# Graph loads one by one, score halves next to each other, three per-graph VectorE operations made per-group GpSimd operations, and separate orders for the first and last group

## The reference

```python
# layer 0
h = x @ W + b;  h = adj @ h / adj.sum(-1)
# layer 1: one weight per node, softmax over the nodes of a graph
w = (q * (adj @ (k * mask))).sum(-1) / sqrt(256);  out = softmax(w)[:, None] * v
# layer 2: attention, 8 heads of 32; the mask is adj + adj
scores = q @ k.T * 32 ** -0.5 * (adj + adj);  out = softmax(scores) @ v @ Wo.T + bo
# layer 3: two hypergraph convolutions, a ReLU and a normalisation between
H = (adj != 0)
m = Be[:, :, None] * (H^T @ (x @ W^T));  out = Dn[:, :, None] * (H @ m) + b
```

## Time and profile before

| | us |
|---|---|
| Median of 3 runs | 1978.1 (1973.22 to 1980.12) |
| Profiled execution | 1963.71 |
| Its span, first to last instruction | 1962.0 |
| PE busy in the span | 1873.0 |
| DVE busy | 1714.7 |
| ACT busy | 1478.6 |
| POOL busy | 1265.0 |

### The profile page before, as it was taken

The page is one execution under the profiler, slowest core; times in us unless marked ns, Lnnn a source line. Parts: engine busy times, 40 slices in busy tenths (PEclk is TensorE's granted clock), DMA queues, the critical chain, the costliest instruction groups (busy, mean ns, idle before and its releaser), DMA issues.

```text
span 1962.0 us, 53573 instructions
## 1 busy us (share of the span) xinstructions
PE 1873.0 (95%) x15357; PEld 1630.5 (83%) x15357; DVE 1714.7 (87%) x4867; ACT 1478.6 (75%) x4431; POOL 1265.0 (64%) x2568
## 2 busy tenths in 40 slices
...
DMA packets 57546, 46.14 MB, mean 24 GB/s; under 512 B 5168, under 2 KB 56880, under 8 KB 57520
## 3 DMA queue, kind: packets, MB, share of 16 engines
...
q10 hardware_dynamic: 1760, 1.90, 0.3%
...
## 4 chain that ended last, share of the span: by engine, by line
PE 78%; DMA 5%; issue 5%; DVE 4%; POOL 4%; ACT 2%; SPq 1%; DVEq 0%; POOLq 0%; ACTq 0%
PE ps L340 38%; PE ps L403 7%; PE ps L443 6%; PE ps L411 6%; DMA a_in<-in_adj_dram 4%; PE ps L419 4%; PE ps L324 4%; PE ps L432 4%; PE ps L356 3%; PE ps L392 3%; POOL ln_rs L653 2%; PE ps L350 1%; DVE x2T L732 1%; PE ps L330 1%; ACT y_out L508 1%
## 5 line engine op out<-in xcount | busy, mean ns | idle before, releaser
L564 ACT ACTIVATE z<-z,z_max 128x128 f32<-128x128 f32 x1024 | 399.1, 398 | 7.2 <-DVE z_max L840 3.1
L653 POOL TENSOR_TENSOR ln_rs<-ln_ve,minus_half 128x1 f32<-128x1 f32 x640 | 360.8, 564 | 50.2
L674 POOL TENSOR_TENSOR z<-z,z_rcp 128x1024 f32<-128x1024 f32 x128 | 242.8, 1897 | 192.9 <-DVE z_rcp L847 192.9
L651 POOL TENSOR_TENSOR ln_ve<-ln_mv,eps_col 128x1 f32<-128x1 f32 x640 | 131.1, 205 | 192.7 <-DVE ln_mv L722 192.7
L656 POOL TENSOR_SCALAR ln_nm<-ln_mv,ln_rs 128x1 f32<-128x1 f32 x640 | 179.7, 281 | 109.8 <-POOL ln_rs L653 109.8
L829 DVE SCALAR_TENSOR_TENSOR z<-ps,a_hold 128x256 f32<-128x256 f32 x512 | 190.5, 414 | 61.4 <-PE ps L403 56.7
L340 PE MATMUL ps<-w1T,txT 128*128 128x512 f32 x768 | 205.0, 402 | 1.0 <-DVE txT L732 1.0
L340 PE MATMUL ps<-w2T,mnT 128*128 128x256 f32 x1536 | 202.3, 284 | 0.1
L564 ACT ACTIVATION_READ_ACCUMULATOR z<-z,z_max 128x1 f32 x1024 | 199.7, 195 | 0.0
L340 PEld LDWEIGHTS ps<-w2T,mnT 128*128 128x128 f32 x1536 | 185.6, 189 | 0.3 <-issue 0.3
L840 DVE TENSOR_REDUCE z_max<-z 128x4 f32<-128x512 f32 x256 | 172.3, 673 | 2.2
(11 more groups left out here) (149 smaller groups left out, 5092.4 us busy)
## 6 DMA issues: line engine op xcount, KB each, us to landing
x_in<-in_x_dram SPq DMA_DIRECT2D x32, 512.0 KB, 4.0
out_dram<-y_out SPq DMA_DIRECT2D x128, 128.0 KB, 1.7
a_in<-in_adj_dram SPq DMA_DIRECT2D x32, 256.0 KB, 2.8
x<-in_L_gnn_Wqk_dram ACTq DMA_DIRECT2D x1, 512.0 KB, 5.6
h<-in_L_gnn_W_dram SPq DMA_DIRECT2D x1, 512.0 KB, 5.3
h<-in_L_gnn_W_dram ACTq DMA_DIRECT2D x1, 512.0 KB, 10.4
v<-in_L_gnn_Wo_dram SPq DMA_DIRECT2D x1, 256.0 KB, 6.2
b_all<-in_L_gnn_b_dram SPq DMA_DIRECT2D x2, 128.0 KB, 8.2
```

Source lines behind the costliest of these rows:

```text
L564: m = act.activation(z[:, g % 2, h, :], z[:, g % 2, h, :], ACT.Exp, bias=z_max[:, g % 2, h:h + 1], accum_out=z_sum[:, g % 2, h:h + 1])
L651: pool.tensor_tensor(ve[n][:, g:g + 1], mv[n][:, g, 1:2], eps_col[:, :], ALU.add).then_inc(eps_made[n], 1)
L653: pool.tensor_tensor(rs[n][:, g:g + 1], ve[n][:, g:g + 1], minus_half[:, :], ALU.pow).then_inc(root_made[n], 1)
L674: pool.tensor_tensor(zg, zg, z_rcp[:, g % 2, :].unsqueeze(2).to_broadcast([P, HEADS, P]), ALU.mult)\
```

## The change

Inputs and the copy of adj are loaded with one DMA for each graph: four for adj (64 KB each), four for x (128 KB each), and four that bring adj a second time, twice over, into `a_hold` with its new form of two equal halves, so that DVE makes no copy. In a round SP issues 16 DMAs, before 6. The score products run with c outside and k inside, and in the new order of PE `sc0` and `sc1` of graphs 0, 1 and 3 stand directly behind each other. DVE reads one half out of PSUM with one instruction over 512 elements. Masking, scaling and the mask's own copy become one GpSimd instruction for a group each (`am`, `hb`, `mask`), and GpSimd makes a constant of the residual for a group with two instructions over 1024 elements (`c3`); DVE's `x3b` is then one instruction for a graph. All orders are new; `v2.0` moves from the end of a round into the next one, `mp.0` to `mp.2` to its start, and `hyper` from its end to its middle. The first and the last group have orders and banks of their own.

The core of the diff:

```diff
     "pe": """
-        at.0+:3 at.1+:6 at.2+:2 sc0.0:0 mp.0:3 ax.0+:4 ax.1+:5 at.3+:7 sc1.0:2 v2.1:6 sc1.1:0 ax.2+:7
...
+        mp.0:7 mp.1:0 mp.2:1 at.0+:6 sc0.0:4 sc1.0:2 at.1+:0 at.2+:6 at.3+:1 ax.0+:7 ax.1+:0 v2.0:1 sc0.1:3
+        sc1.1:5 h0.0+:2 mp.3:7 ax.2+:3 sc0.2:5 ax.3+:7 v2.1:0 h0.1+:4 pt.0:1 h0.2+:3 sc1.2:4 cx.0:6 x1t.0+:1
...
-ORDER = {engine: steps(text) for engine, text in ORDER_TEXT.items()}
-FIRST = {engine: [s for s in schedule if s[2] == 1] for engine, schedule in ORDER.items()}
-LAST = {engine: [s for s in schedule if s[2] == 0] for engine, schedule in ORDER.items()}
+ORDER, FIRST, LAST = ({engine: steps(text) for engine, text in texts.items()}
+                      for texts in (ORDER_TEXT, FIRST_TEXT, LAST_TEXT))
...
             def load_a(q, g):
-                after(sp, made["at"], q * G)
+                after(sp, made["at"], before(q, g, G))
                 after(sp, a_summed, q)
-                after(sp, a_held, q)
-                sp.dma_start(a_in[:, :, :], adj_d[bass.ds(q * G, G)].rearrange("g n m -> n g m")).then_inc(a_loaded, 16)
+                sp.dma_start(a_in[:, g, :], adj_d[bass.ds(q * G + g, 1)].rearrange("g n m -> n (g m)")).then_inc(a_loaded[g], 16)
+
+            def load_hold(q, g):
+                after(sp, read["sc0"], before(q, g, G))
+                after(sp, read["sc1"], before(q, g, G))
+                sp.dma_start(a_hold[:, g, :, :], adj_d[bass.ds(q * G + g, 1)].rearrange("g n m -> n g m").to_broadcast([P, C, P]))\
+                    .then_inc(hold_loaded[g], 16)
...
             def sc(half):
                 def stage(q, g, o, b):
-                    if g == 0:
-                        for s in ("q0", "q1", "k0", "k1"):
-                            pe.wait_ge(read[s], q + 1)
-                    for k in range(RG // 2):
-                        r = half * RG // 2 + k
-                        at_ = slice(r * HD, (r + 1) * HD)
-                        for c in range(C):
+                    for s in ("q0", "q1", "k0", "k1"):
+                        pe.wait_ge(read[s], q + 1)
+                    for c in range(C):
+                        for k in range(RG // 2):
+                            r = half * RG // 2 + k
+                            at_ = slice(r * HD, (r + 1) * HD)
                             m = pe.matmul(ps[:, b + k, c * P:(c + 1) * P], qT[at_, c, g * P:(g + 1) * P],
                                           kT[at_, c, g * P:(g + 1) * P], start=True, stop=True)
...
+            def am(q, g):
+                pool.wait_ge(mask_made, q + 1)
+                pool.wait_ge(read["at"], nth(q, G - 1))
+                after(pool, made["amx"], q * G)
+                pool.tensor_tensor(amT[:, :, :], aT[:, :, :], mask[:, :].unsqueeze(2).to_broadcast([P, G, P]), ALU.mult)\
+                    .then_inc(amT_made, 1)
...
+            def c3_(q, g):
+                pool.wait_ge(d_made, q * 2 + 2)
+                after(pool, x3b_made, q * G)
+                pool.tensor_tensor(c3[:, :, :], bw_all[:, :].unsqueeze(1).to_broadcast([P, G, D]),
+                                   d_cnt[:, :].unsqueeze(2).to_broadcast([P, G, D]), ALU.mult).then_inc(c3_half, 1)
+                pool.wait_ge(c3_half, q + 1)
+                pool.tensor_tensor(c3[:, :, :], c3[:, :, :], b2_all[:, :].unsqueeze(1).to_broadcast([P, G, D]), ALU.add)\
+                    .then_inc(c3_made, 1)
...
             def asum(q, g, o):
-                dve.wait_ge(a_loaded, q * 16 + 16)
-                after(dve, wm_made, q)
-                dve.tensor_copy(mask[:, :], maskT[:, bass.ds(q * G, G)]).then_inc(mask_made, 1)
+                for k in range(G):
+                    dve.wait_ge(a_loaded[k], q * 16 + 16)
...
+                    dve.scalar_tensor_tensor(out=z[:, g % 2, hs, :].rearrange("p (r c) n -> p r (c n)", r=RG // 2),
+                                             in0=ps[:, b:b + RG // 2, 0:C * P], scalar=HC,
+                                             in1=a_hold[:, g, :, :].rearrange("p c n -> p (c n)").unsqueeze(1)
+                                             .to_broadcast([P, RG // 2, C * P]),
+                                             op0=ALU.mult, op1=ALU.mult).then_inc(read[f"sc{half}"], 1)
...
-            def x3c_(q, g, o):
-                dve.wait_ge(x3b_made, nth(q, g))
-                dve.wait_ge(d_made, q * 2 + 2)
-                dve.scalar_tensor_tensor(out=x3b[:, g, :], in0=bw_all[:, :], scalar=d_cnt[:, g:g + 1], in1=x3b[:, g, :],
+            def x3b_(q, g, o):
+                dve.wait_ge(norm_made["ln2"], nth(q, g))
+                dve.wait_ge(c3_made, q + 1)
+                after(dve, norm_made["ln4"], before(q, g, G))
+                dve.scalar_tensor_tensor(out=x3b[:, g, :], in0=x3[:, g, :], scalar=2.0, in1=c3[:, g, :],
                                          op0=ALU.mult, op1=ALU.add).then_inc(x3b_made, 1)
```

More of the change, by code:

```diff
@@ L56 @@
+        q1.0+ ln4_norm.3
     """,
     "dve": """
-        asum.0+ sc0.0 zmax0.0 sc1.0 zmax1.0 ax_lo.0+ sc1.1 ax_lo.1+ zmax1.1 zrcp.0 sc0.1 h0.0+ zmax0.1
-        ax_lo.2+ ln0_stats.0+ h0.1+ ln0_aggr.0+ ln0_stats.1+ sc0.2 zrcp.1 sc1.2 zmax0.2 ax_lo.3+ cx_lo.0
-        h0.2+ ln0_aggr.1+ zmax1.2 wo.0 ln0_stats.2+ ln2_stats.0 ln2_aggr.0 sc0.3 am.0+ sc1.3 zrcp.2 h0.3+
-        x1t_lo.0+ zmax0.3 am.1+ ln0_aggr.2+ ln0_stats.3+ tx_lo.0 dinv.0 ln0_aggr.3+ zmax1.3 cx_lo.1 am.2+
-        xg.0+ h1.0 x1t_lo.1+ wo.1 zrcp.3 am.3+ cx_lo.2 hold.0+ ln2_stats.1 xg.1+ ln2_aggr.1 x1t_lo.2+ wo.2
@@ L68 @@
-        x2t_lo.1+ y.2 x2t_lo.2+ ln4_stats.2 x2t_lo.3+ ln4_aggr.2 y.3 ln4_stats.3 ln4_aggr.3 hyper.0+
+        asum.0+ z0.0 zmax0.0 z1.0 ax_lo.0+ zmax1.0 z0.1 z1.1 zmax1.1 zrcp.0 ax_lo.1+ zmax0.1 h0.0+
+        ln0_stats.0+ ax_lo.2+ h0.1+ ln0_aggr.0+ z0.2 zrcp.1 h0.2+ zmax0.2 ln0_stats.1+ ln0_stats.2+ ax_lo.3+
+        ln0_aggr.1+ z1.2 cx_lo.0 h0.3+ x1t_lo.0+ ln0_aggr.2+ zmax1.2 wo.0 ln2_stats.0 ln0_stats.3+
+        ln2_aggr.0 z1.3 ln0_aggr.3+ z0.3 zmax1.3 xg.0+ zrcp.2 dinv.0 x1t_lo.1+ cx_lo.1 zmax0.3 x1t_lo.2+
@@ L541, in aT_free @@
                 after(act, made["ax"], before(q, g, G))
-                after(act, amT_made, before(q, g, G))
+                after(act, amT_made, q)
                 after(act, hT_made, q)
```

253 lines of the change are left out of this document (149 added, 104 removed).

## The result

| | median of the runs | span profiled | granted clock |
|---|---|---|---|
| before | 1975.66 us (1965.51 to 1980.12, 4 runs) | 1962.0 | 0.986 |
| changed | 2017.3 us (2016.75 to 2019.3, 4 runs) | 2017.6 | 0.980 |

The ratio is 1.022, 95% interval 1.0178 to 1.0262. The kernel is slower, where 1952 us and a gain of 1.3% were predicted, and the time lies outside the range. The two profiled spans lie 56 us apart and the medians 42, since the profiled execution of the kernel before is faster than its median.

The account below looks back on a forecast made before the run. PE's own queue was taken to set the pace of a round. Minus 0.75 us a round over 31 rounds (minus 23) and minus 3 at the ends took 1978.1 to 1952 us, range 1892 to 1996.

Parts of the forecast that it names:

- From `cx.0` to the next s: Rest of a round until the next first adj load issue (s): same work less two `mp` and a wait, 42.95 us.
- it only makes waits rarer: DVE loses at least 3 of its 53.06 us a round; nothing needs that, as PE is the longer one.
- the race of POOL for `probs.3`: `probs.3` queued behind `c3` on POOL comes 0.3 to 1.3 us late for `pt.3`; taken as 0.
- the 58.15 forecast: Length of a round: 15.2 us to `cx.0` plus 42.95 after it, 0.75 us less than before.
- Landings of 1.9 and 2.2 us: At a round's start, small loads take 1.9 us for 64 KB and 2.2 us for 128 KB, by slope.
- the 2.15 us of the other estimate: 64 KB load time by the skill page's fit; each landing 0.25 us later, 8 us in all.
- the stretch that the prediction summed: Round's start on PE, 4.6 us with 2.7 of work: some 1.9 us idle, against 0.8 in the old order.
- Minus 1.2 us of PE work a round: Score halves on PE: three pairs and two single halves take 3.40 us, where the old order took 4.60.
- the term is wrong: Sign for the score pairs: a pair taking 1.1 us or more would refute the 1.2 us saving.
- Rival 3: `probs.3` or a normalisation root behind `c3` or `hb` on POOL comes 1.5 us late for PE: 1998 us, chance 0.08.
- The ends: Filling and draining parts: minus 1 and minus 2 us, minus 3 in all; bounds plus 3 and minus 10.
- rival 2: Granted clock falls in more rounds, 4.6 us each; six more cancel the gain, ten more give 1998 us; chance 0.17.

Follow-up runs that it names:

- part 2: `hyper` moved to the end of DVE's round, `hb.0` last on POOL, against the changed kernel: 1972.0 us; with `d_inv` early too, 1968.45 us.
- part 1: Against the changed kernel: `d_inv` one place earlier on DVE, 2003.8 us; `hyper` behind `ln2_aggr.3`, 2019.07 us; both, 2018.39 us.
- the kernel of 1968: Changed kernel with `d_inv` one place earlier, `hyper` at the end of DVE's round and `hb.0` last on POOL: 1968.45 us.
- Part 5: Three score pairs taken apart: changed kernel 2217.54 us; with `d_inv` early, `hyper` last, one adj load 2094.75; that load also issued by ScalarE 1965.46.

## Why the prediction was wrong

**The step that failed** is "From `cx.0` to the next s ... The new order has there the same work": 42.95 us were forecast. The rows have 61.13 - 15.09 = 46.04. The two stretches, before and after, in the columns of the earlier trace rows:

```profile
1036.76:1080.28 43.52, 43.15 (x364) 38.29 (x364) 41.58 (x122) 33.65 (x92) 33.83 (x73) 1.00 0.03 10
1057.69:1103.73 46.04, 43.48 (x362) 38.35 (x361) 40.08 (x112) 34.42 (x92) 31.13 (x66) 1.00 0.04 13
```

The prediction took the 58.9 of one round and the `cx.0` of another, which has 43.5 behind it and not 43.9, so its 42.95 should have been 42.6. Of the missing 3.5 us three waits make 2.55: 1.45 ahead of `xg.1`, 0.84 ahead of `xg.3`, 0.26 ahead of `cx.3`. Most of the remainder is work: PE is busy there for 0.33 us more than before, where 0.66 less were forecast; why is open.

That step stood on the sentence that DVE loses work and "it only makes waits rarer". DVE did lose 3 us a round and its waits grew, for two reasons. The change takes `hyper` from the end of DVE's round, where DVE waits for the next loads anyway, to its full middle; the prediction used `hyper` only in the race of POOL for `probs.3` and never asked what stood behind it on DVE. That is 45 us by part 2. And it priced DVE and POOL as if each were alone, while `d_inv` and `hb` come to stand beside POOL's 1.9 and 2.4 us instructions. For `d_inv` that is some 0.8 us of an undisturbed round by part 1, of which falls of the clock took back about half, and 0.2 or nothing once `hyper` is out of the way; freeing `hb` alone gave nothing. The earlier trace rows held the sign: `hb`'s L804 took 744 ns for 128 elements, longer than the 0.68 us of a reduction over 512. In the trace all but four of the 128 take 0.7 to 0.8 us, beside POOL's `x2c` of 0.73 us; the four of the filling part take 0.28. I copied the mean as a price and did not ask why.

With both out of the way (the kernel of 1968) an undisturbed round still takes 59.4 us, 1.2 more than the 58.15 forecast. Half of that is the 0.6 us at `pt.3`, the term that the prediction worked out as POOL being late by 0.3 to 1.3 us and then took as 0. The rest was not traced.

**The loads.** Landings of 1.9 and 2.2 us were forecast, 1.8 and 2.1 came, so not the 2.15 us of the other estimate either; `cx.0` at s + 15.2 was 15.09. The waits of PE in the stretch that the prediction summed are 1.1 us and not 1.9, and three `mp` take 0.81 us, not 0.65 (by its own 0.33 for one they should have been 0.99), but neither sets `cx.0`: the chain through DVE and ScalarE does, as it had worked out. What it did not ask is what this start would take with one load, all else as changed: taking the split back gives 35 us, of which falls of the clock, two in place of fifteen, are some 7. The split itself was no gain, since `a_sum` waits for all four loads and heads DVE's order, while x is issued behind them.

**The pairs.** The term "Minus 1.2 us of PE work a round" was for two pairs more than before. Part 5 takes three pairs apart: 2.0 and 1.9 us, where the prediction's rows make 1.8. So the price of a pair holds. In the changed kernel less of it is seen: a new pair holds PE for 1.01 or 1.07 us to the next start, the third for 0.67, and with two halves alone, 0.65 each, that is 4.05 us by the time line of that round against the 4.60 of before; PE's busy time in a round fell by 0.1 us. The rows of 1.08 and 1.14 us were also the sign that was to mean "the term is wrong", and it was a bad sign: no other part that was tested costs as much when it is taken back (200 us on the changed kernel, against 106 for `c3`). Why the experiments give a pair more than its rows is open.

**POOL and fill and drain.** `c3` takes 4.3 us in one piece (3.8 to 4.8 forecast), and `pt.3` did not wait for POOL in the changed kernel, but only because PE was held up ahead of it. Rival 3 had the sign right with the wrong chain, POOL holding DVE and not PE. The ends were forecast at minus 3 and gave minus 8.6 in the span; undoing their orders costs 12.

**The clock (rival 2).** Fifteen rounds hold a fall, 12 more than before, and by the prediction's price of 4.6 us that alone would have made it slower. But each lasts 3.4 us, not 10.2, and costs some 0.7 (61.8 against 61.1): 11 us in all, less than the 14 of before. The count came as that rival had it, and its price was wrong.
